# One more GpSimd drain in the routed stage of a fused token, attention and expert kernel

## What is computed

```python
    scores = jax.nn.softmax(logits, axis=-1)
    topk_w, topk_i = _group_limited_topk(scores)          # 2 of 8 experts for each row
    wmat = (jax.nn.one_hot(topk_i, N_EXPERTS, dtype=topk_w.dtype) * topk_w[..., None]).sum(axis=1)
    g = jnp.einsum('th,nfh->ntf', h, gate_w)
    u = jnp.einsum('th,nfh->ntf', h, up_w)
    e = jnp.einsum('ntf,nhf->nth', jax.nn.silu(g) * u, down_w)
    routed = jnp.einsum('nth,tn->th', e, wmat)
    sg = h @ sh_gate_w.T
    su = h @ sh_up_w.T
    shared = jax.nn.silu(sg) * su @ sh_down_w.T
    return (routed + shared).reshape(B, S, H)
```

## Time and profile before

| what | value |
|---|---|
| median of three runs | 863.58 us |
| span of the profiled execution, first to last instruction | 856.7 us |
| PE busy over the span | 87% |
| DVE, POOL, ACT busy | 60%, 41%, 36% |
| routed stage, about | 505 to 845 us |
| last scatter issued | 845.0 us |
| stream of GpSimd ends | 856.6 us |

### The profile page before, as it was taken

One profiled execution on the slowest core, in us unless ns is written; L12 is line 12 of the kernel. 1 busy time (PEld: TensorE's weight loads), 2 busy tenths in 40 slices (PEclk: granted clock), 3 DMA queues, 4 the chain that ended last, 5 costly groups with the idle time before them and its releaser, 6 DMA issues.

```text
span 856.7 us, 18955 instructions
## 1 busy us (share of the span) xinstructions
PE 745.3 (87%) x6717; PEld 465.7 (54%) x6718; DVE 513.0 (60%) x929; ACT 309.8 (36%) x582; POOL 347.0 (41%) x359
## 2 busy tenths in 40 slices
PE   0006999879889999999999999999999999999992
PEld 0006999655436454555545545665665656656551
DVE  7996764867786474856875533554444444444441
ACT  4782432525225253435333412333223223223231
POOL 0027683343065021210037753555545545455432
PEclk9999999999999999999999999999999999999997
DMA  5010225325272314296562528898976777677752
GB/s 213 0 49 27 77 66 181 109 76 103 67 185 37 93 61 140 86 218 149 157 153 51 156 65 207 168 157 129 143 138 120 143 135 131 138 136 129 126 99 37
DMA packets 126894, 99.73 MB, mean 116 GB/s; under 512 B 95889, under 2 KB 96017, under 8 KB 126321
## 3 DMA queue, kind: packets, MB, share of 16 engines
q1 hardware_dynamic: 99344, 43.64, 22.8%
q0 software_dynamic: 14240, 30.06, 19.3%
q10 hardware_dynamic: 13248, 25.17, 10.6%
HBM read 48.46 MB, written 28.15 MB: 89 GB/s over the span
## 4 chain that ended last, share of the span: by engine, by line
PE 72%; DVE 12%; ACT 5%; DMA 4%; POOL 2%; issue 2%; SPq 2%; ACTq 0%; DVEq 0%; POOLq 0%
PE PS L2159 12%; PE PS L2160 12%; PE PS L2161 12%; PE PS L607 7%; PE PS L1105 6%; PE PS L1107 6%; PE PS L1106 6%; PE PS L765 3%; PE PS L2182 2%; SPq L1877 2%; DVE work L1470 1%; DVE big L1465 1%; DMA work<-in_shared 1%; PE PS L1260 1%; DMA big<-x_dram 1%
## 5 line engine op out<-in xcount | busy, mean ns | idle before, releaser
L2159 PE MATMUL PS<-big,work 128*128 x493 | 165.7, 336 | 4.7 <-DMA work<-big 2.7
L2160 PE MATMUL PS<-big,work 128*128 x493 | 165.7, 336 | 0.0
L2161 PE MATMUL PS<-big,work 128*128 x493 | 165.7, 336 | 0.0
L2331 POOL DMA_INDIRECT out_dram<-work x55 | 88.1, 1602 | 120.1 <-DVE work L2299 54.6
L2224 ACT ACTIVATE work<-PS 128x768 f16<-128x768 f16 x55 | 44.6, 810 | 165.5 <-PE PS L2182 165.5
L2273 DVE SCALAR_TENSOR_TENSOR work<-work 128x352 f16<-128x352 f32 x55 | 32.1, 584 | 89.8 <-ACT work L2231 89.8
L1714 POOL DMA_INDIRECT slots_dram<-work x48 | 48.9, 1019 | 81.2 <-DVE work L2075 62.8
L2315 POOL DMA_INDIRECT big<-x_dram,work x55 | 55.5, 1009 | 45.4 <-POOL work L2312 45.4
L2159 PEld LDWEIGHTS PS<-big,work 128*128 128x128 f16 x493 | 48.4, 98 | 39.6 <-issue 6.1
L2161 PEld LDWEIGHTS PS<-big,work 128*128 128x128 f16 x493 | 48.4, 98 | 36.1
L2160 PEld LDWEIGHTS PS<-big,work 128*128 128x128 f16 x493 | 48.3, 98 | 33.4
(11 more groups left out here) (286 smaller groups left out, 1680.0 us busy)
## 6 DMA issues: line engine op xcount, KB each, us to landing
big<-in_weights ACTq DMA_DIRECT2D x33, 272.0 KB, 3.5
work<-in_weights ACTq DMA_DIRECT2D x31, 272.0 KB, 3.1
work<-in_shared ACTq DMA_DIRECT2D x28, 256.0 KB, 3.1
x_dram<-big SPq DMA_DIRECT2D x24, 256.0 KB, 2.3
out_dram<-big SPq DMA_DIRECT2D x24, 256.0 KB, 2.9
big<-in_par SPq DMA_DIRECT2D x1, 1185.0 KB, 10.4
big<-in_c_real SPq DMA_DIRECT2D x1, 1024.0 KB, 5.6
big<-in_c_imag SPq DMA_DIRECT2D x1, 1024.0 KB, 7.5
```

What stands on the lines that cost most here:

```text
L2159: pe.matmul(out, x_high, w_high, start=start, stop=False)
L2160: pe.matmul(out, x_high, w_low, start=False, stop=False)
L2161: return pe.matmul(out, x_low, w_high, start=False, stop=stop)
L2331: pool.indirect_dma_start(out_d, bass.IndirectOffsetOnAxis(ap=S_NUM[u][:, 0:1], axis=0), YO[u], None, compute_op=ALU.add).then_inc(s_add[u ...
```

## The change

In the written-out last tiles, GpSimd gets one drain. The condition is true once, at t = 50 (50 + 5 = 55), so the drain stands behind gather 54 and scatter 49 and ahead of the five last scatters, 50 to 54.

```diff
             for t in range(4 * turns + 4, SLOT_TILES):
                 if t + ahead < SLOT_TILES:
                     gather(0, t + ahead)
+                elif t + ahead == SLOT_TILES:
+                    pool.drain()
                 scatter(0, t)
```

## The result

The changed kernel took 858.08 us in the median of ten runs, the kernel before 863.21 us in ten. The ratio is 0.9939, with a 95% interval of 0.9918 to 0.9959: 5.3 us less, between 3.5 and 7.1. The forecast was 857.8 us, and the drop forecast was 5.75 us.

What follows compares the result with a forecast made beforehand. PE sets the pace in the routed stage, POOL's 6.08 us closing drain bounds the end. Span 856.7 - 5.75 + 0 = 850.95 us; with 6.9 us outside, 863.58 - 5.75 = 857.8 us, range 857.2 to 864.6.

Steps and rivals of the forecast that it cites:

- What bounds the end: Last 12 us: POOL's closing drain takes 6.08 us with nothing beside it; every nanosecond it loses, the end gains.
- first of the two readings: POOL's drain goes one by one through DMAs issued since the last drain, 37 ns each; 5.75 us go at the end.
- middle case: At tile 50: drain starts at 820.63, takes 5.9 us to 826.5; scatter 50 goes 3.1 us late, no delay at the end.
- high case: At tile 50: drain first sees scatter 49 land, ends at 830.3; scatter 50 6.5 to 7.5 us late, end 0 to 0.9.
- wrong in the cover: Sign at the tail: scatter 50 after 831, result of tile 52 waiting for DMA, scatter 54 later than 845.0.
- the price taken, nothing: Drain at tile 50 costs 0 us at the end, covered by 4 us of POOL waiting and 0.81 us of DVE idling.
- The part outside of the span: Measured time beyond the profiled span of 856.7 us: 6.9 us, left as it is.
- The fee for each drain: Rival: closing drain keeps its 6.08 us with any DMA; time 863.6, up to 864.7; chance 0.33, including no effect.
- The drain that is dearer in its place than at the end: Rival: traffic at 820 to 824 us holds the new drain at tile 50; over 0.2% (1.7 us) slower; chance 0.05.
- T = 829.9: Drain's end at tile 50 past which DVE's result of tile 52 runs past 836.47; each later microsecond is one at the end.

Runs made afterwards that it cites:

- e2_filler: Changed kernel with its new drain replaced by one semaphore increment that nobody waits for, at the same place: 0.9994 of the kernel before.
- e3_two_at_end: Kernel before with a second drain directly ahead of the closing one: a single run took 864.95 us, median of the kernel before 864.97.
- e4_early_only: Kernel before with one drain behind the first five gathers and none at tile 50: 0.9990 of the kernel before.
- e6_late_53: Changed kernel with its drain moved from ahead of scatter 50 to ahead of scatter 53: 0.9986 of the kernel before.

## Why the prediction was right

**What bounds the end.** Right. The 6.08 us of the closing drain had nothing beside them, and `e2_filler` and `e3_two_at_end` leave both the drain's work and the time where they were. What went off the closing drain went off the tail, but for the delay below.

**What the drain does.** The first of the two readings was right in kind: it goes through DMAs, and those that an earlier drain has settled aren't gone through again (40 ns in `e3_two_at_end`). Its size was not right. 6079 / 164 = 37 ns was a mean over a curve with a ceiling. For a drain that starts with DMAs in flight the curve rises by 0.041 us for each DMA and stops at some 4.4 us behind the landing; for one that starts with all landed it rises by about 0.08 ((4.40 - 0.47) / 48, from 5 DMAs to 53) and is at 5.7 to 6.2 us from 105 on. For the change as it stands that cost nothing, because 159 were settled and 5 left: the closing drain kept 0.57 us where I had said 0.19 to 0.36. The gain at the end was 5.51 us, by 0.24 less than my 5.75. Moved to another place, the same arithmetic would have failed, as `e4_early_only` did: 0.34 us instead of 2.1.

**What it costs where it stands.** I had taken the middle case, in which the drain starts as soon as POOL is free; it was the high one. The drain waits for scatter 49 to land. It ended 11.0 and 9.6 us after the issue of scatter 49, for which the high case had 830.3 - 819.03 = 11.3. Inside it the landing took 6.6 and 5.2 us instead of 5.4, and the rest 4.38 instead of 5.9, so in the first profile two errors offset each other. From the drain's end to the issue of scatter 50 it was 1.55 us, for which the prediction had taken 1.5. (Its 0.84 us between a copy and an issue came from a row that ended with a DMA; a row without one, that of scatter 51 above, has 0.80.) The consequence was the one named: scatter 50 came late, the result of tile 52 waited for it, and the product of tile 54 behind it came late, so that the result of tile 54 was delayed by 1.3 us in one profile and by nothing in the other. Its bound was 0.9 us. What was mis-sized is the landing of scatter 50. The 4.3 us were read from the end of its traffic, but the last update of its semaphore came 4.75 us after its issue in the kernel before already, and 5.08 and 4.75 in the changed kernel's two profiles; DVE started 0.16 us after that. In the first profile that makes 5.2 us, 0.9 more than was taken.

By its own signs the prediction was wrong in the cover in the first profile: the result of tile 52 waited for a DMA, scatter 50 went at 837.96, which is 831.6 in before's time (with the issue of scatter 49 at the same place), and scatter 54 came 1.3 us later after the result of tile 50 than before. In the second profile only the wait for the DMA is there. That the price taken, nothing, was still nearly right is in part luck: the case that it was taken from didn't occur, and in the one that did, the idle time on POOL and DVE swallowed most of the drain.

**The sum.** 5.51 us off the closing drain less 0 to 1.3 us of delay is 4.2 to 5.5; the measured drop is 5.3 (3.5 to 7.1). The tails of the two profiles fell by 0.3 to 0.5 us more than that, since what stands around the closing drain (the landing of scatter 54, the drain's start, the barrier) took that much less than in the one profile of before. Kernels that keep the long closing drain differ by as much: 33.1 to 33.7 us of tail in five profiles. The forecast of 5.75 lies in the interval, a little high, because it took the delay as nothing.

**The part outside of the span.** I had put it at 6.9 us, from the span of one execution and the median of others. In each later run that lists both, time and span differ by 1.7 to 1.8 us (859.57 and 857.8). By that the profiled execution of before took some 858.4 us (an estimate: 856.7 + 1.7), less than any of the ten whose times are listed. The sum used differences alone, so this didn't reach the forecast, but the table ahead of the prediction should not be read as if the two belonged together.

**The rivals.** The fee for each drain is out by the 566 ns and the 40 ns. The drain that is dearer in its place than at the end was half there: 9.9 to 11.2 us against 6.1. What it took beyond its rest of 4.38 us, the same in both profiles, is the wait for the landing. In before's time, with the issue of scatter 49 at the same place, it ended at 830.1 in the first profile, just past the point at which it starts to cost (T = 829.9), and at 828.7 in the second, ahead of it. `e6_late_53` shows what such a drain does at tile 53, where nothing absorbs it: it gives back most of what the end gains. The rule of the Trainium skill's page "VectorE: DVE Perf Modes", section "The DRAIN you can't avoid", that the drains around a kernel are constant boilerplate of about 12 ns on all engines, doesn't hold for GpSimd here: 40 ns to 6.16 us, by the DMAs behind it.

## What to carry to other kernels

Read the last microseconds of a program on the sequencers, not on the engines: an instruction there that runs with nothing beside it is worth its full time. In this kernel GpSimd's closing drain is paid for DMAs issued long before (6.08 us for 164), and an earlier drain takes that over. Such a drain belongs where GpSimd idles, with enough tiles behind it to absorb what a landing and the settling take beyond that idle time (9.9 to 11.2 us here, with 4 us idle), and seldom enough that the landing it waits for isn't paid again and again.

## What the runs showed that I had not expected

The settling has a ceiling: with 107, 159 and 162 DMAs since the last drain, 4.4 to 4.5 us remain after the last landing, and closing drains with 111 and 164 take 6.14 and 6.08 to 6.16. What sets the ceiling no run here shows. Open too is why a drain that starts with all landed takes some 0.08 us for each DMA up to 53 and one that starts with DMAs in flight half of that. The 53 were mostly slot writes, and with all landed I didn't try the kinds apart; with DMAs in flight the table shows no difference between them.

The spread of single runs is made mostly ahead of the routed stage, as far as the profiles show: in the fourteen of this study the result of tile 0 started anywhere between 529 and 542 us, whereas from there to tile 50 it took 293.2 to 294.3 us in every kernel without a drain in the loop. A change of a few microseconds in this stage is read better from such a stretch than from two spans.
